# Routed third feed-forward: tile stages two to four tiles apart, deeper rings, second banks for two turns

## The reference, cut to what matters

```python
logits = jnp.einsum('bsd,de->bse', x, Wg)
top_vals, top_idx = jax.lax.top_k(logits, TOP_K)
probs = jax.nn.softmax(top_vals, axis=-1)
...
for e in range(E):
    u = jnp.einsum('bsd,dh->bsh', x, W1[e])
    v = jnp.einsum('bsd,dh->bsh', x, W2[e])
    h = u * jax.nn.sigmoid(u) * v
    y = jnp.einsum('bsh,hd->bsd', h, W3[e])
    out = out + y * weights[..., e][..., None]
```

## Time and profile before

| what | before |
|---|---|
| median of three runs | 1105.28 us |
| lowest, highest | 1103.7, 1110.93 us |
| the profiled execution | 1108.78 us |
| its span on the core | 1107.0 us |
| mean granted TensorE clock over the span | 0.92 |
| TensorE busy in the span | 931.5 us (84%) |
| VectorE, ScalarE, GpSimd busy | 601.3, 499.6, 300.9 us |
| first turn-in to last y copy of the tile stage | 883.71 to 1015.67 us |

### The profile page before, as it was taken

The page is one execution under the profiler, slowest core; times in us unless marked ns, Lnnn a source line. Parts: engine busy times, 40 slices in busy tenths (PEclk is TensorE's granted clock), DMA queues, the critical chain, the costliest instruction groups (busy, mean ns, idle before and its releaser), DMA issues.

```text
span 1107.0 us, 12051 instructions
## 1 busy us (share of the span) xinstructions
PE 931.5 (84%) x3714; PEld 425.8 (38%) x3714; DVE 601.3 (54%) x1207; ACT 499.6 (45%) x937; POOL 300.9 (27%) x303
## 2 busy tenths in 40 slices
PE   5799999999799999998767984957877776887788
PEld 2344545454222222332233761422332344554433
DVE  2223233433888878777224445379998542545355
ACT  4233223233267667777632331665755421445720
POOL 9100000000001110110363561056756645433010
PEclk9799999999899999999969996988988886988889
DMA  8660000040011211210232206000000201311023
GB/s 175 183 235 0 1 1 1 1 93 0 23 52 49 77 49 51 59 43 3 55 105 70 56 26 189 8 11 1 0 1 7 69 28 53 100 33 50 3 77 114
DMA packets 81329, 59.52 MB, mean 54 GB/s; under 512 B 23422, under 2 KB 75704, under 8 KB 81172
## 3 DMA queue, kind: packets, MB, share of 16 engines
q1 hardware_dynamic: 74932, 51.00, 16.8%
q0 software_dynamic: 6336, 7.77, 2.3%
HBM read 38.41 MB, written 21.87 MB: 54 GB/s over the span
## 4 chain that ended last, share of the span: by engine, by line
PE 62%; DVE 12%; issue 11%; ACT 7%; another core or an unknown queue 2%; POOL 2%; SPq 2%; DMA 2%; DVEq 0%; POOLq 0%; ACTq 0%
PE psum L853 59%; ACT sb_scr L1884 3%; DVE sb_scr L2604 3%; DVE sb_scr L2979 2%; DVE sb_scr L2988 2%; POOL sb_scr L800 1%; ACT sb_qstack L1884 1%; ACT psum L1884 1%; SPq L629 1%; PE psum L1684 1%; PE psum L1009 1%; PE psum L1661 1%; SPq L634 0%; DVE sb_scr L2466 0%
## 5 line engine op out<-in xcount | busy, mean ns | idle before, releaser
L1884 ACT ACTIVATE sb_scr<-psum 128x512 f32<-128x512 f32 (+5 forms) x592 | 298.6, 539 | 367.1 <-PE psum L853 243.2
L2604 DVE TENSOR_REDUCE sb_scr<-psum 128x2 f32<-128x1024 f32 x128 | 154.7, 1222 | 40.3 <-PE psum L853 40.0
L761 POOL DMA_DIRECT2D sb_heads<-sb_scr x48 | 24.8, 523 | 439.6 <-DVE sb_scr L2620 439.3
L853 PE MATMUL psum<-sb_wide,sb_scr 128*128 (+1 forms) x532 | 120.8, 356 | 7.0 <-DVE sb_scr L3141 5.5
L800 POOL TENSOR_TENSOR sb_scr<-sb_scr 128x512 f32<-128x512 f32 x64 | 82.7, 1298 | 99.0 <-ACT sb_scr L1884 53.1
L853 PE MATMUL psum<-sb_kstack,sb_qstack 96*128 96x512 bf16 x256 | 98.2, 395 | 8.2 <-DVE sb_scr L2604 8.1
L853 PE MATMUL psum<-sb_qstack,sb_kstack 128*128 128x512 bf16 x256 | 99.0, 393 | 4.2 <-ACT sb_scr L1884 2.8
L2530 DVE TENSOR_SCALAR sb_scr<-psum,sb_b 128x512 f32<-128x512 f32 x48 | 34.6, 748 | 116.4 <-PE psum L853 116.4
L1884 ACT ACTIVATE sb_scr<-psum,sb_b 128x512 f32<-128x512 f32 x48 | 31.3, 685 | 142.9 <-PE psum L853 142.9
L853 PE MATMUL psum<-sb_h,sb_wide 128*128 128x512 f32 x192 | 88.3, 596 | 0.8 <-ACT sb_scr L1884 0.8
L853 PEld LDWEIGHTS psum<-sb_wide,sb_scr 128*128 128x128 f32 x532 | 76.4, 202 | 30.4 <-issue 28.5
(11 more groups left out here) (338 smaller groups left out, 1367.0 us busy)
## 6 DMA issues: line engine op xcount, KB each, us to landing
sb_qstack<-q_bounce SPq DMA_DIRECT2D x48, 96.0 KB
sb_kstack<-k_bounce SPq DMA_DIRECT2D x144, 32.0 KB
sb_scr<-pick_rows SPq DMA_DIRECT2D x8, 512.0 KB
sb_scr<-tiles_in SPq DMA_DIRECT2D x22, 129.0 KB
expert_in<-sb_scr SPq DMA_DIRECT2D x4, 645.0 KB, 6.1
tiles_in<-sb_scr SPq DMA_DIRECT2D x4, 645.0 KB, 8.3
sb_scr<-expert_in SPq DMA_DIRECT2D x8, 322.5 KB, 3.5
expert_out<-sb_scr SPq DMA_DIRECT2D x4, 512.0 KB, 4.9
```

Source lines behind the costliest of these rows:

```text
L761: pool.dma_start(heads[at:at + DH, b % 2, :], head_out(n)[32 * j:32 * j + DH, :]).then_inc(sem(f"heads_packed{b % 2}"), 16)
L853: return nc.tensor.matmul(out_, w, r, start=start, stop=stop, **kw)
L1884: return nc.scalar.activation(out_, in_, func, **kw)
L2604: v.reduce_max(headmax[:, g % 2, t:t + 2, j], banks, AX.X).then_inc(sem("maxed"), 1)
```

## The change

The stages of a tile are moved apart. In round c TensorE now issues turn-in c+2, up c, hidden turn c-2 and down c-4, over 50 rounds. ScalarE's round is copy-in c+2, gate c; VectorE's is product c, hidden copy c-2, y copy c-4. `xT2_in` gets three places, `hid2` and `hidT2` four each. The turn-in of odd tiles 8 to 22 goes to bank 6 instead of 0 and their hidden turn to bank 7 instead of 3; all other tiles keep the one bank. The bank of down, `x2_in`, `y2_rows`, the gate's two places and GpSimd's and SyncE's streams stay. The first half's combination and what follows up to the variances move by one or two rounds, and the second half's words are read in rounds 5 to 7.

```diff
-        xT2_in = view(14352, 2 * P).rearrange("p (r t) -> p r t", r=2)
-        gact2 = view(14608, 2 * H2).rearrange("p (r f) -> p r f", r=2)
+        xT2_in = view(14352, 3 * P).rearrange("p (r t) -> p r t", r=3)
+        gact2 = view(14736, 2 * H2).rearrange("p (r f) -> p r f", r=2)
...
-        hid2, hidT2 = (view(at, 2 * H2).rearrange("p (r f) -> p r f", r=2) for at in (6144, 6656))
+        hid2, hidT2 = (view(at, 4 * H2).rearrange("p (r f) -> p r f", r=4) for at in (4096, 5120))
...
+        def in2_bank(c):
+            return 6 if 8 <= c < TILES2 and c % 2 else 0
+
+        def hid2_bank(c):
+            return 7 if 8 <= c < TILES2 and c % 2 else 3
+
+        def last_use(bank_of, c):
+            return next((n for n in reversed(range(c)) if bank_of(n) == bank_of(c)), None)
...
             def turn_in2(c):
                 pe.wait_ge(*tile_loaded(c))
-                if c >= 1:
-                    pe.wait_ge(sem("xT1_ready"), NSTEP + c)
-                nc.tensor.transpose(psum[:, 0, 0:P], x2_in[:, y2_place(c)[1], 0:D], eye[:]).then_inc(sem("x1_turned"), 1)
+                before_it = last_use(in2_bank, c)
+                if before_it is not None:
+                    pe.wait_ge(sem("xT1_ready"), NSTEP + before_it + 1)
+                if in2_bank(c) == 6:
+                    pe.wait_ge(sem("h_rows_ready"), NB + 4)
+                nc.tensor.transpose(psum[:, in2_bank(c), 0:P], x2_in[:, y2_place(c)[1], 0:D], eye[:]).then_inc(sem("x1_turned"), 1)
...
             def turn_hidden2(c):
                 pe.wait_ge(sem("hid2_ready"), c + 1)
-                if c >= 1:
-                    pe.wait_ge(sem("hidT2_ready"), c)
+                before_it = last_use(hid2_bank, c)
+                if before_it is not None:
+                    pe.wait_ge(sem("hidT2_ready"), before_it + 1)
                 for k in range(2):
-                    m = nc.tensor.transpose(psum[:, 3, k * P:(k + 1) * P], hid2[:, c % 2, k * P:(k + 1) * P], eye[:])
+                    m = nc.tensor.transpose(psum[:, hid2_bank(c), k * P:(k + 1) * P], hid2[:, c % 4, k * P:(k + 1) * P], eye[:])
...
-                if c in (10, 13, 16):
-                    load_word(1, (c - 10) // 3)
+                if c in (5, 6, 7):
+                    load_word(1, c - 5)
                 for b in range(2):
                     at = 6 + b
-                    if n == 6 + b:
+                    if n == 8 + b:
                         turn_back2(b, at)
-                    if n == 8 + b:
+                    if n == 9 + b:
                         center3(b, at)
-                    if n == 10 + b:
+                    if n == 11 + b:
                         variance3(b, at)
...
             turn_in2(0)
-            for c in range(NTILE2 + 2):
-                if c + 1 < NTILE2:
-                    turn_in2(c + 1)
+            turn_in2(1)
+            for c in range(NTILE2 + 4):
+                if c + 2 < NTILE2:
+                    turn_in2(c + 2)
                 if c < NTILE2:
                     blocks[c] = block_of(c)
                     up2(c)
-                if 1 <= c < NTILE2 + 1:
-                    turn_hidden2(c - 1)
-                if c >= 2:
-                    down2(c - 2)
+                if 2 <= c < NTILE2 + 2:
+                    turn_hidden2(c - 2)
+                if c >= 4:
+                    down2(c - 4)
                 beside_tiles(c)
...
-                    if n == 5 + b:
+                    if n == 7 + b:
                         combine2(b)
-                    if n == 7 + b:
+                    if n == 8 + b:
                         add_batch2(b, at)
...
-            for c in range(NTILE2 + 2):
+            for c in range(NTILE2 + 4):
                 if c < NTILE2:
                     product2(c)
-                if 1 <= c < NTILE2 + 1:
-                    copy_hidden2(c - 1)
-                if c >= 2:
-                    copy_y2(c - 2)
+                if 2 <= c < NTILE2 + 2:
+                    copy_hidden2(c - 2)
+                if c >= 4:
+                    copy_y2(c - 4)
                 beside_tiles(c)
```

More of the change, by code:

```diff
@@ L1675, in up2 @@
                     pe.wait_ge(sem("hid2_ready"), c - 2)
-                mm(bank(UP2_BANKS[c % 3]), xT2_in[:, c % 2, :], WIDE[:, bass.ds(blocks[c], 2 * H2)]).then_inc(sem("up2_done"), 1)
+                mm(bank(UP2_BANKS[c % 3]), xT2_in[:, c % 3, :], WIDE[:, bass.ds(blocks[c], 2 * H2)]).then_inc(sem("up2_done"), 1)
             def turn_hidden2(c):
                 pe.wait_ge(sem("hid2_ready"), c + 1)
-                if c >= 1:
-                    pe.wait_ge(sem("hidT2_ready"), c)
+                before_it = last_use(hid2_bank, c)
+                if before_it is not None:
+                    pe.wait_ge(sem("hidT2_ready"), before_it + 1)
                 for k in range(2):
-                    m = nc.tensor.transpose(psum[:, 3, k * P:(k + 1) * P], hid2[:, c % 2, k * P:(k + 1) * P], eye[:])
+                    m = nc.tensor.transpose(psum[:, hid2_bank(c), k * P:(k + 1) * P], hid2[:, c % 4, k * P:(k + 1) * P], eye[:])
                 m.then_inc(sem("hid2_turned"), 1)
@@ L1692, in down2 @@
                 for k in range(2):
-                    m = mm(psum[:, 4, 0:D], hidT2[:, c % 2, k * P:(k + 1) * P],
+                    m = mm(psum[:, 4, 0:D], hidT2[:, c % 4, k * P:(k + 1) * P],
                            WIDE[:, 2 * H2 + k * D:][:, bass.ds(blocks[c], D)], k == 0, k == 1)
@@ L2229, in copy_in2 @@
                 act.wait_ge(sem("x1_turned"), NSTEP + c + 1)
-                if c >= 2:
-                    act.wait_ge(sem("up2_done"), c - 1)
-                f(xT2_in[:, c % 2, :], bank(0, P), ACT.Copy).then_inc(sem("xT1_ready"), 1)
+                if c >= 3:
+                    act.wait_ge(sem("up2_done"), c - 2)
+                f(xT2_in[:, c % 3, :], bank(in2_bank(c), P), ACT.Copy).then_inc(sem("xT1_ready"), 1)
             def gate2(c):
@@ L2320, in beside_tiles @@
                     at = 6 + b
-                    if n == 9 + b:
+                    if n == 10 + b:
                         copy_and_square3(b, at)
@@ L2344, in _ @@
             copy_in2(0)
+            copy_in2(1)
             for c in range(NTILE2):
-                if c + 1 < NTILE2:
-                    copy_in2(c + 1)
+                if c + 2 < NTILE2:
+                    copy_in2(c + 2)
                 gate2(c)
@@ L3122, in product2 @@
                 dve.wait_ge(sem("gact2_ready"), c + 1)
-                if c >= 2:
-                    dve.wait_ge(sem("hid2_turned"), c - 1)
-                v.tensor_tensor(hid2[:, c % 2, :], psum[:, UP2_BANKS[c % 3], H2:2 * H2], gact2[:, c % 2, :], ALU.mult).then_inc(sem("hid2_ready"), 1)
+                if c >= 4:
+                    dve.wait_ge(sem("hid2_turned"), c - 3)
+                v.tensor_tensor(hid2[:, c % 4, :], psum[:, UP2_BANKS[c % 3], H2:2 * H2], gact2[:, c % 2, :], ALU.mult).then_inc(sem("hid2_ready"), 1)
             def copy_hidden2(c):
                 dve.wait_ge(sem("hid2_turned"), c + 1)
-                if c >= 2:
-                    dve.wait_ge(sem("down2_done"), c - 1)
-                v.tensor_copy(hidT2[:, c % 2, :], bank(3, H2)).then_inc(sem("hidT2_ready"), 1)
+                if c >= 4:
+                    dve.wait_ge(sem("down2_done"), c - 3)
+                v.tensor_copy(hidT2[:, c % 4, :], bank(hid2_bank(c), H2)).then_inc(sem("hidT2_ready"), 1)
             def copy_y2(c):
```

## The result

The changed kernel has a median of 1113.8 us over 12 runs (1108.88 to 1116.76), the kernel before 1105.42 over 12. The ratio is **1.0059, interval 1.0042 to 1.0076**: by it 6.5 us slower, where the prediction had 5.2. (The two medians lie 8.4 us apart, and the forecast time was 1110.) In a later group of runs the ratio was 1.0050 (1.0019 to 1.0081). The profiled execution took 1111.06 us, only 2.3 more than that of before, because its stage begins 4.2 us earlier (turn-in 0 at 879.53 instead of 883.71). So I compare times counted from turn-in 0.

The account below looks back on a forecast made before the run. GpSimd was taken to set the pace from 900 to 940, TensorE's own work the full-speed rounds. Terms 4.2 + 1.8 - 0.7 + 2.5 - 3.8 + 1.2 gave +5.2 on 1105.28, forecast 1110 us, range 1101 to 1117.

Parts of the forecast that it names:

- GpSimd later by 2.9: Start of the routed stage: y(3) leaves two rounds later, delaying GpSimd's burst and all y behind it by 2.9 us (0 to 4.3).
- No gain from the second banks in 900 to 937: Stretch with late results: down's single bank keeps TensorE within a round of VectorE, so late results cost the same; gain 0.
- -0.7 for quicker full-clock rounds: Full-speed rounds: hidden turn no longer waits for VectorE's product, 1.74 falls towards 1.65 over 8 rounds, -0.7 us (0 to -1.1).
- New wait of 4.9 before turn-in 23: Tile 23's load waits until tile 15 is scattered; TensorE idles 4.9 us, making round 21 4.2 us late.
- Restart at half clock, +1.8: After the idle time before turn-in 23, TensorE restarts at 1.2 GHz, costing 1.8 us (0 to 3).
- Wait before turn-in 31, +2.5: Tile 31's load waits until tile 22 is scattered, adding 2.5 us and making round 29 7.8 us late in all.
- The combination later, -3.8: Rounds 29 to 37: VectorE's wait for gathered rows falls from 2.98 to about 1; 28.6 us becomes 24.8, -3.8.
- The end, +1.2: Stage end: five downs remain after up 45 instead of three, so recur3 is ready 1.2 us later (0 to 2.6).
- A: Rival for the late-result stretch: GpSimd cannot hold TensorE's results, the deeper pipeline covers the latency; faster, 1102 us; 12%.
- B: Rival at the loads: no new wait, early lag hidden, gain of the rounds and the end cancel; 1105 us; 23%.
- C: Rival between tiles 3 and 15: GpSimd starves three times instead of two, 3 + 6 us more; 1119 us; 10%.

Follow-up runs that it names:

- group 3: Follow-up runs on one chip with late results: both kernels once more and two scatter tests; before 1109.76 us, changed kernel 1114.82 us, ratio 1.0050.
- down7_after: Changed kernel with the second bank of odd tiles 8 to 22 given to down instead of the hidden turn: 1095.21 us, ratio 1.0087 to before.
- x24_after: Changed kernel with 23 places for loaded tiles instead of 16: 1106.16 us, ratio 0.9954 to the kernel before.
- lag2: Changed kernel with hidden turn one round and down two rounds behind up, as before: 1106.0 us, ratio 0.9964 to the kernel before.
- early_after: Changed kernel with GpSimd's scatters of the second half's rows from tile 1 on instead of tile 3: 1115.11 us, ratio 1.0040 to before.
- moved_before: Kernel before with only the first half's combination and what follows it moved one or two rounds later: 1080.67 us, ratio 0.9954 to before.
- group 1: Follow-up runs on one chip with late results, four variants of the changed kernel; the kernel before had a median of 1109.92 us there.
- group 2: Follow-up runs on one chip where no TensorE result is late, four variants; the kernel before had a median of 1086.37 us there.
- x24_before: Kernel before with 23 places for loaded tiles instead of 16 and nothing else: 1080.97 us, ratio 0.9945 to before.
- noscatter: Kernel before without GpSimd's sixteen scatters of the second half's rows: 1089.26 us in one run.
- busy: Kernel before with a GpSimd multiplication in place of each of the sixteen scatters of the second half's rows: 1094.51 us in one run.

## Why the prediction was right, step by step

The sign, the place and the new wait were right, and the sum was 1.3 below the measured 6.5. That it came so close is in part luck: several terms were off and offset each other. The numbers are those of the first profiled pair; the pair of group 3 stands at the end of the list.

- **GpSimd later by 2.9: mis-sized.** Tile 3 was scattered 5.6 later (15.3 to 20.9), above the upper bound of 4.3. I had taken two rounds as 3.5, the turn-in as 0.8, and 1.4 off for lighter first rounds. Product 3 comes 1.4 later, and y(3) 8.3 after it instead of 4.1: two rounds cost 4.2, and the 1.4 were not there. y(15) moved 3.9, more than the 2.9, less than 5.6; GpSimd's three waits from tile 7 on were 1.0 shorter in sum. In the pair of group 3 tile 3 was scattered 5.0 later and y(15) came 5.2 later.
- **No gain from the second banks in 900 to 937: no speedup seen, its reason untested.** Results stayed late (turn-ins 13, 14 and 18 by 3.1, 8.1, 6.3; before 10, 11 and 15 by 4.7, 7.4, 8.7). That down's bank is the tie wasn't settled by down7_after. The -0.7 for quicker full-clock rounds can't be separated.
- **New wait of 4.9 before turn-in 23: right,** 4.55 in the row, 4.8 beyond a normal round; chain 5.82 against 6.0; round 21 5.1 late against 4.2. x24_after removes it and lag2 shrinks it to 0.91, in two different ways.
- **The wait before turn-in 16: left out.** The list of loads in the prediction begins with tile 23, but tile 16's waits for the result of tile 7, which is now three rounds ahead of its turn-in instead of six. TensorE stood 1.74 for it in this execution, not at all in the other of after, and 5.49 and 11.27 in early_after and down7_after.
- **Restart at half clock, +1.8: right,** 3.31 at a granted clock of 0.54 instead of 1.65.
- **Wait before turn-in 31, +2.5: right,** 2.46 in the row; round 29 was 9.2 late against 7.8.
- **The combination later, -3.8: mis-sized in this pair.** Its wait went to 0, not 1, and the rounds with the combinations took 3.4 each instead of 4.6. Rounds 29 to 37 took 22.7 instead of 24.8, a gain of 5.9. moved_before measured 5.0 for this part alone. Round 37 was 3.3 late against 4.0, and nothing was added up to gate 45 (3.2 late).
- **The end, +1.2: right for its step.** y(45) is 2.6 later behind gate 45 and `project_out3` 1.07. The second half's 32 turn-backs follow `project_out3` without idle time in both kernels, but take 4.97 at a mean granted clock of 0.76 instead of 3.95 at 0.94, and the next norm's first matmul comes 18.55 behind gate 45 instead of 16.33, 2.2 later. In the pair of group 3 this clock term is smaller (4.86 at 0.77 against 4.42 at 0.84) and the norm comes 1.8 later. What the end costs in all isn't settled: 3.3 in the first pair, 0.3 in the other. Behind gate 45 before takes 95.0 in one execution and 97.9 in another, after 98.3 and 98.2.

In sum for the profiled pair: 5.1 (round 21) + 4.1 to round 29 - 5.9 + 0 + 3.3 = 6.6, against 6.5 from turn-in 0 to the end. The pair of group 3 has 6.4 + 5.3 - 3.9 - 1.2 + 0.3 = 6.9 for the same stretches. The total repeats, and so do the waits before turn-ins 23 (4.54) and 31 (2.42); single terms differ by up to 3, and the combination's is -3.9 there, against the -3.8 of the forecast. By the ratios, the moved combination gives back some 5 and the lag over 16 places costs some 11, measured on different chips.

**Rivals.** A (late results go away) fell: they are there in both executions of after, and in all its variants of group 1. The Trainium skill's SBUF — State Buffer, section on the two separate sides, has TensorE never wait on anyone. That is about ports, and no run here shows a wait at one, so the traces don't contradict it. It was the step from there to results in time that failed: with GpSimd's DMAs taken away they are on time, and TensorE is busy for 19.0 of 20 us. On the chip where none is late, before itself is 19 us faster than its first median, and down7_after, the nearest to the change that ran there, is slower than it: a kernel with the longer lag does not gain there either. B (no new wait) fell by turn-in 23's row. C (a third starvation) didn't occur: GpSimd waits at tiles 7 and 11 as before.

## What to carry to other kernels

When stages are moved apart, every ring that the last stage frees has to grow by the distance, not only those next to the moved stage: here three rings got deeper, and the ring of the loads, which wait for the last stage's result, did not. That turned two rounds of lag into 9 us of waits and slow restart. Follow every group of the ring, the first refill too. Price the lag by the slow first rounds (4.2 here, not 3.5) and the drain, not by the steady round. And try the parts alone: a consumer moved two rounds behind its gather paid 5 us and needed none of the rings.

## What the runs showed of the hardware

- Chips differ in whether TensorE's results are held up. In the first measurement and on the chips of groups 1 and 3 they come up to 9.7 us late while GpSimd issues indirect DMAs 1.28 us apart, and the kernel before takes 1105 to 1110 us. On the chip of group 2 no result is late beside the same stream, and it takes 1086. The mean granted clock is about the same (0.92, and 0.93 for x24_before). Why is open.
- Where results are late, the DMAs stood back to back. Beside scatters mostly 1.6 us and more apart (noscatter), or with 1.75 us of multiplications between them (busy), none was late on a chip that has the delay.
- The last 95 to 98 us behind gate 45 vary by 3 us between executions of one kernel, and TensorE's granted clock in the stretch from 40 to 50 us behind it varies with them (0.67 in the shorter execution of before, 0.50 in the longer). A term of that size can't be read from one pair of traces.
